# A two-layer gated cross-attention and expert kernel: the maxima are turned ahead of the scores, and routing work changes steps

## The reference

```python
x = x + tanh(g_xattn[0]) * L0_xattn(layernorm(x), ctx, Wq, Wkv, Wo)
x = x + tanh(g_ffn[0])   * L0_ffn(layernorm(x), gate_w, w1, w2)            # top-2 of 8, gelu
x = x + tanh(g_xattn[1]) * L1_xattn(layernorm(x), ctx, ctx, Wq, bq, ...)   # with biases
x = x + tanh(g_ffn[1])   * L1_ffn(layernorm(x), Wr, br, W1, b1, W2, b2)    # top-2 of 8, relu, norm
```

## Time and profile before

| | |
|---|---|
| median of 3 runs | 573.4 us (572.22 to 574.28) |
| the profiled execution's own time | 571.19 us |
| its span, first to last instruction | 569.4 us |
| mean granted TensorE clock | 0.826 of full |
| PE busy | 440.4 us (77%) |
| DVE busy | 336.9 us (59%) |
| ACT busy | 214.2 us (38%) |
| POOL busy | 237.4 us (42%) |
| DMA, mean over the span | 56 GB/s |

### The profile page before, as it was taken

The page is one execution under the profiler, slowest core; times in us unless marked ns, Lnnn a source line. Parts: engine busy times, 40 slices in busy tenths (PEclk is TensorE's granted clock), DMA queues, the critical chain, the costliest instruction groups (busy, mean ns, idle before and its releaser), DMA issues.

```text
span 569.4 us, 16851 instructions
## 1 busy us (share of the span) xinstructions
PE 440.4 (77%) x5346; PEld 334.9 (59%) x5350; DVE 336.9 (59%) x1255; ACT 214.2 (38%) x608; POOL 237.4 (42%) x378
## 2 busy tenths in 40 slices
PE   7788889878576899999478787877865799999300
PEld 4465455545444699998145555544544699999300
DVE  4678556755438656666338855754544756666493
ACT  4434323232232444442044432323221566666221
POOL 7023543453443144445102354435345244554456
PEclk9599785978855999999869968677875999999855
DMA  7791000000000122221200010000010122222241
GB/s 222 213 314 22 21 20 2 22 21 20 20 18 25 47 67 67 70 65 52 74 10 21 20 39 30 4 18 21 20 50 28 42 57 68 63 68 65 70 121 55
DMA packets 38672, 32.06 MB, mean 56 GB/s; under 512 B 6984, under 2 KB 32245, under 8 KB 38613
## 3 DMA queue, kind: packets, MB, share of 16 engines
q1 hardware_dynamic: 34069, 21.86, 14.0%
q0 software_dynamic: 4544, 9.41, 5.1%
HBM read 20.26 MB, written 10.99 MB: 55 GB/s over the span
## 4 chain that ended last, share of the span: by engine, by line
PE 53%; DVE 20%; issue 8%; another core or an unknown queue 8%; ACT 3%; POOL 3%; DMA 2%; DVEq 1%; POOLq 1%; ACTq 0%; SPq 0%
PE bank L671 49%; PE bank L674 4%; DVE room L1288 4%; DVE mx L1265 4%; ACT room L1052 2%; DVE room L1295 1%; DMA o_rows<-room,ids 1%; DVE v_s L1167 1%; POOL wa L648 1%; DVE x L1250 1%; DVE x L1302 1%; DVE wa L1497 1%; DVE fstats L1307 1%; DVE wa L1490 1%
## 5 line engine op out<-in xcount | busy, mean ns | idle before, releaser
L623 POOL DMA_INDIRECT o_rows<-room,ids x78 | 77.7, 996 | 101.0 <-DVE room L1438 37.2
L671 PE MATMUL bank<-room 128*128 128x128 f32 x624 | 83.8, 277 | 2.9 <-issue 2.0
L671 PE MATMUL bank<-wa,room 128*128 x624 | 83.0, 276 | 1.3 <-ACT room L1110 1.1
L671 PEld LDWEIGHTS bank<-room 128*128 128x128 f32 x624 | 75.7, 192 | 6.1 <-ACT room L1115 3.1
L671 PEld LDWEIGHTS bank<-wa,room 128*128 128x128 f32 x624 | 76.1, 192 | 2.0 <-issue 1.9
L576 POOL DMA_INDIRECT xg_rows<-xfa,slots x64 | 63.9, 998 | 32.0 <-issue 19.0
L1265 DVE TENSOR_REDUCE mx<-bank 128x4 f32<-128x324 f32 x128 | 54.4, 487 | 36.2 <-PE bank L671 36.2
L988 ACT ACTIVATE room<-bank 128x128 f32<-128x128 f32 (+1 forms) x110 | 31.2, 284 | 107.2 <-PE bank L674 104.7
L1288 DVE RECIPROCAL room<-bank 128x128 f32<-128x128 f32 x32 | 30.6, 956 | 60.6 <-remote 47.4
L1052 ACT ACTIVATE room<-bank 128x384 f32<-128x384 f32 x128 | 52.4, 495 | 27.0 <-PE bank L671 27.0
L1415 DVE COPY room<-wa 128x512 f32 x78 | 33.3, 427 | 39.2 <-issue 20.3
(11 more groups left out here) (191 smaller groups left out, 733.9 us busy)
## 6 DMA issues: line engine op xcount, KB each, us to landing
room<-xg_rows SPq DMA_DIRECT2D x78, 65.5 KB
wa<-in_L_ffn_w SPq DMA_DIRECT2D x1, 2048.0 KB, 10.1
wb<-in_L_ffn_W SPq DMA_DIRECT2D x1, 2048.0 KB, 17.1
ob<-o_rows SPq DMA_DIRECT2D x32, 64.0 KB, 1.9
wb<-o_rows SPq DMA_DIRECT2D x6, 256.0 KB, 4.5
o_rows<-room,ids POOLq DMA_INDIRECT x78
x<-in_x SPq DMA_DIRECT2D x4, 256.0 KB, 4.4
xg_rows<-xfa,slots POOLq DMA_INDIRECT x64
```

Source lines behind the costliest of these rows:

```text
L623: pool.indirect_dma_start(out=o_dram[l], in_=o_sb[t.slot(UN)][:, :], in_offset=None, out_offset=bass.IndirectOffsetOnAxis(ap=ids[t.slot(UN ...
L671: return pe.matmul(out_, lhsT, rhs, start=start, stop=stop)
```

## The change

On PE: `turn_max` now stands ahead of `scores`, and `less_max` right behind it; the transpose of `xn` stands ahead of `wo`; logits and more_values stand behind `wo`; ranks are made in even steps. On DVE: `ons` directly follows the reciprocal; the ranks and the logits are read out of bank 7 early in the step, and `place` (even steps) and `choose` (odd steps) stand at its end; the later values of a step are kept in the next step; both statistics of a pair are taken together in the even step. On POOL: a pair is scattered at s = b+8 (odd) and no more at b+7 (even); the pair 13 stays at s = 20 and the pair 15 at s = 21, now both through `placed`. The core of the diff:

```diff
+        def due(s, n, last):
+            if s.c == B - 1 + last:
+                return Step(B - 1)
+            return Step(s.c - n) if live_pair(s.back(n)) and s.c - n < B - 1 else None
+        def chosen(s):
+            return due(s, 6, 5)
+        def placed(s):
+            return due(s, 7, 6)
@@ POOL step (in front: xfa of the pair s-4 in odd steps, rstd in even steps)
-                    if live_pair(b6):
+                    if placed(s):
                         ... cum += mb, twice, behind the wait for rk
-                    ready = b6 if b6.c == B - 1 else b7
-                    if live_pair(ready) and (ready.c == B - 1) == (ready is b6):
-                        S["f4"].wait(pool, ready)
...
+                    for b in [b8] * (live_pair(b8) and b8.c < B - 3) + [placed(s)] * (s.c >= B + 4):
+                        S["f4"].wait(pool, b)
+                        S["f2"].wait(pool, b)
+                        scatter(b, 0)
+                        scatter(b, 1)
@@ PE step
-                    if live_pair(b5):
+                    if placed(s):
+                        ranks(placed(s), s)
+                    if live_pair(b5) and b5.c == B - 1:
                         logits(b5)
-                    if live_pair(b6):
-                        S["f3"].wait(pe, b6, 8)
...
-                    if l == 0:
-                        more_values(s)
                     if live(b2):
+                        turn_max(b2)
                         scores(b2)
-                        turn_max(b2)
+                        less_max(b2)
+                    if live(s):
+                        S["xn"].wait(pe, s)
+                        tr(bank[4][:, NC * T:NC * T + P], xn[s.slot(2)][:, :], P).then_inc(S["t1"].sem, 1)
                     if live(b3):
                         ... wo
-                    if live(b2):
-                        less_max(b2)
...
+                    if live_pair(b5) and b5.c < B - 1:
+                        if placed(s):
+                            S["f4"].wait(pe, placed(s), 1)
+                        if l == 0:
+                            pe.wait_ge(v_kept, min(s.c + 1, B))
+                        logits(b5)
+                    if l == 0:
+                        more_values(s)
                     if live_pair(b4):
                         S["f2"].wait(pe, b4)
                         if l == 0:
-                            pe.wait_ge(v_kept, min(s.c + 2, B))
-                        S["f4"].wait(pe, b4.back(2), 1)
+                            pe.wait_ge(v_kept, min(s.c + 1, B))
+                        if chosen(s):
+                            S["f3"].wait(pe, chosen(s), 1)
@@ DVE step
                         dve.reciprocal(...)
-                    if l == 0 and late_batch(s.c) is not None:
-                        ... values_kept(late_batch(s.c))
                         ... ons
+                    if placed(s):
+                        if chosen(s):
+                            S["lg"].wait(dve, chosen(s))
+                        read_ranks(placed(s))
+                    if chosen(s):
+                        read_logits(chosen(s))
+                    if l == 0 and late_batch(s.c - 1) is not None:
+                        ... values_kept(late_batch(s.c - 1))
                     ... norm statistics of s+2, update of x
+                    if live_pair(b3):
+                        ... bn_stats twice, bn_aggr twice
+                    if placed(s):
+                        place(placed(s))
+                    if chosen(s):
+                        choose(chosen(s))
```

More of the change, by code:

```diff
@@ L864, in logits, with ranks @@
                     ins.then_inc(S["lg"].sem, 1)
+                def ranks(b, s):
+                    S["f3"].wait(pe, b, 8)
+                    S["cu"].wait(pe, b.back(2))
+                    if live_pair(s.back(5)):
+                        S["c2"].wait(pe, s.back(5))
+                    if l == 0 and b.c == 1:
+                        hear(pe, "consts")
+                    r0, r1 = bank[7][:, 272:280], bank[7][:, 280:288]
+                    mm(r0, tri[:, :], mb[:, 0, :], True, False)
+                    mm(r0, onesb[:, :], cum[:, :], False, True)
+                    mm(r1, tri[:, :], mb[:, 1, :], True, False)
+                    mm(r1, onesb[:, :], mb[:, 0, :], False, False)
+                    mm(r1, onesb[:, :], cum[:, :], False, True).then_inc(S["rk"].sem, 1)
                 def step(s):
-                    b1, b2, b3, b4, b5, b6 = (s.back(n) for n in (1, 2, 3, 4, 5, 6))
+                    b1, b2, b3, b4, b5 = (s.back(n) for n in (1, 2, 3, 4, 5))
                     if live(b2):
@@ new lines, in choose @@
+                def choose(b):
+                    f3, two = S["f3"], xfa[:, b.c - 1:b.c + 1, D + 1:D + 3]
+                    if l == 0 and b.c == 1:
+                        hear(dve, "consts")
+                    f3.wait(dve, b, 1)
+                    for j in range(2):
+                        dve.max(top[:, j, :], lg[:, j, :]).then_inc(f3.sem, 1)
+                    f3.wait(dve, b, 3)
+                    for j in range(2):
+                        dve.max_index(topi[:, j, :], top[:, j, :], lg[:, j, :]).then_inc(f3.sem, 1)
+                    f3.wait(dve, b, 5)
+                    dve.tensor_copy(two, topi[:, :, 0:2]).then_inc(f3.sem, 1)
+                    f3.wait(dve, b, 6)
+                    S["f4"].wait(dve, b.back(2))
+                    ohv = oh[:, :, :].rearrange("p (j k) e -> p j k e", k=2)
+                    dve.tensor_tensor(ohv, iota8[:, :].unsqueeze(1).unsqueeze(1).to_broadcast([P, 2, 2, E]),
+                                      two.unsqueeze(3).to_broadcast([P, 2, 2, E]), ALU.is_equal).then_inc(f3.sem, 1)
+                    f3.wait(dve, b, 7)
+                    S["cu"].wait(dve, b.back(2))
+                    dve.tensor_tensor(mb[:, :, :], ohv[:, :, 0, :], ohv[:, :, 1, :], ALU.add).then_inc(f3.sem, 1)
+                    dve.tensor_tensor(gap[:, b.c - 1:b.c + 1], top[:, :, 1], top[:, :, 0], ALU.subtract).then_inc(f3.sem, 1)
@@ new lines, in read_ranks, with place @@
+                def read_ranks(b):
+                    S["rk"].wait(dve, b)
+                    dve.tensor_tensor(rk[:, :, :], bank[7][:, 272:288].rearrange("p (j e) -> p j e", j=2),
+                                      bc3(regoff[:, :], 2), ALU.add).then_inc(S["f4"].sem, 1)
+                def place(b):
+                    f4, c = S["f4"], b.c
+                    f4.wait(dve, b, 1)
+                    dve.tensor_tensor(pick[:, :, :].rearrange("p (j k) e -> p k j e", k=2),
+                                      oh[:, :, :].rearrange("p (j k) e -> p k j e", k=2),
+                                      rk[:, :, :].unsqueeze(1).to_broadcast([P, 2, 2, E]), ALU.mult)\
+                        .then_inc(f4.sem, 1)
+                    f4.wait(dve, b, 2)
+                    with nc.allow_low_precision(reason="row numbers, exact in float32 and int32"):
+                        dve.tensor_reduce(slots[:, c - 1:c + 1, :].rearrange("p j k -> p (j k)"), pick[:, :, :],
+                                          AX.X, ALU.add).then_inc(f4.sem, 1)
@@ L1303, in step @@
                                                  ALU.mult, ALU.add).then_inc(S["x2"].sem, 1)
[L1304 removed]
+                    if live_pair(b3):
+                        f1 = S["f1"]
                         S["x2"].wait(dve, b3)
[L1306 to L1311 removed]
```

95 lines of the change are left out of this document (25 added, 70 removed).

## The result

The changed kernel takes **530.46 us** (median of 4 runs, 528.16 to 537.93) where the kernel before takes 573.19 beside it (4 runs, 572.22 to 574.28): ratio **0.924**, 95% interval 0.919 to 0.930. The forecast was 565 (552 to 579); the sign is right, the size is five times too small. The profiled execution is the longest of the four: 537.93, span 535.9, against 571.19 and 569.4. Stretches are read from it. They add up to 7.5 us more than the median tells.

A forecast was written before the change was run, and what follows sets the result against it. Attention was taken as bound by a PE, DVE and ACT chain, its PE part paid at two clocks, with holds at scatters. Layer 0 -5.4 and layer 1 -3.4, together -8.8 from 573.4, gave 565 us, range 552 to 579.

The forecast's parts named there:

- the hold: While POOL issues scatters, PE's results reach other engines late, coming free about 1.0 us behind the last scatter.
- the steps with a scatter: Attention: scatters start about 3.5 us in; only the exponentials wait; next step at 10.4 against 10.77, bounds 8 and 12.
- the exponentials escape: Faster rival, chance 0.13: in scatter steps the exponentials run before the hold; a pair costs 16.5, total 549 us.
- pairs: Two attention steps, one with a scatter: forecast 18.4 us in layer 0 and 18.5 in layer 1.
- s = 17 to `frs` of pair 15: Last scatter step plus clean s = 18: 10.1 and 5.4 us in layer 0, 10.4 and 5.2 in layer 1.
- First steps: Clean steps s = 3 to 7: earlier turn saves 0.7 us each in layer 0, 0.55 in layer 1; -3.5 and -2.7.
- Clean steps between scatters: Attention steps without scatter: early rank reads take 8.5 us to about 8.0 in layer 1, bounds 7.6 and 8.5.
- The tail: After `frs` of pair 15: an extra scatter group costs +3.7 us in layer 0 and +7.5 in layer 1.
- POOL's `rstd` behind four scatters: `rstd` for the next steps queues behind four scatters: costed at nothing, up to 1 us a pair if steps are shorter.
- The slower rival: Chance 0.20: scatter steps beginning at 1.2 GHz let the hold catch the turn; next step at about 11.9, total 580 us.
- does not come from the scatters: Rival, chance 0.07: the hold belongs to PE's own queue at even steps; pairs keep their 10.8 step, about 560 us.

The follow-up runs named there:

- the turn alone: Kernel before with only the maxima turned ahead of the scores and less_max behind them: 556.54 us, ratio 0.970; on another chip 506.43, ratio 0.982.
- the deferred kernel: Changed kernel with all scatters of pairs 1 to 11 held back to step 20: 557.99 us, ratio 0.970; on another chip 550.57, ratio 1.079.

## Why the prediction was wrong

**The step that failed is the place of the hold's beginning, in "the steps with a scatter".** I took it within about 1 us of the first indirect DMA: reciprocal and turn would be out, the exponentials stand behind it, 10.4 for the step. In the traces the lateness grows through the row of four. What PE ends 0.8 behind the first still gets out, 0.6 to 2.0 late; the update of x, whose product ends 1.3 behind, starts 3.5 behind in five of the eight rows of after; most of what PE ends 1.6 or more behind waits for the end of the hold. The odd steps took 7.9 on the mean for 10.4, and this is nearly all of the error in the pairs. The trace of before had both cases, in the step of the earlier trace rows, in rows that I did not weigh (ACT and PE there):

```profile
348.73 1.10 POOL L576 DMA_INDIRECT xg_rows<-xfa,slots  x1 [0.46 <-issue]
349.09 0.49 PE L671 MATMUL bank<-xnT,wq 128*128 128x128 f32 x2
349.50 0.86 PE L671 MATMUL bank<-room,keep 128*32 128x128 f32 x24
...
350.82 0.37 ACT L1064 ACTIVATE room<-bank,bqs 128x128 f32<-128x128 f32 x1 [2.76 <-PE bank L671]
...
351.33 0.63 PE L671 MATMUL bank<-room,kz 32*128 32x128 f32 x9 [0.43 <-issue]
```

The query product ends at 349.58, 0.85 behind the first scatter, and ACT has it at 350.82, in the midst of the row of four and 1.24 late; the weights end at 350.36, 1.63 behind, and are the ones held to 354.62. My own sum put the end of less_max at 0.9 behind the scatter, so by these rows it escapes. That is the rival "the exponentials escape", and its chance of 0.13 should have been the forecast's. On the profiled scale the forecast was 562.4 and 537.7 came (span and 1.8), 24.7 less: pairs -21.1 (58.8 and 67.7 for 73.6 and 74.0), s = 17 to `frs` of pair 15 -4.0 (13.6 and 13.5 for 15.5 and 15.6), first steps -3.1, tails +2.4, small terms about +1. The rival's 16.5 a pair was near in layer 1 (mean 16.9, granted clock 0.81) and too high in layer 0 (14.7, clock 0.88).

**First steps**: right in mechanism, -3.9 and -5.4 for -3.5 and -2.7. 5.48 for 5.7; the bound of 0.85 was passed by a little (0.92), since less_max starts 0.77 behind the scores (41.63, 42.40) and not 0.88. In layer 1 two steps of before that last 8.3 and 7.6 went down to 6.6 and 5.5 as well.

**Clean steps between scatters**: 8.0 was forecast and 7.9 came, by luck, because the hold has moved into these steps. The wait of the earlier trace rows is gone, and the turn alone shows what it would have cost (0.83).

**The tail**: the sum is near, +13.6 for +11.2, the split is wrong. In layer 0 I let PE's keys and values hide the group; they are held themselves, as the products of 0.72 us above are, and end at 159.4: +8.7, above my bound of +5, where the chip without the hold shows +3.5. In layer 1 `cum` of pair 15 comes 13.7 behind its `frs` (forecast 16.1, though the parts listed there add up to 15.6): no hold shows in that tail, and pair 13 is placed at 399.8, while the scatters of pair 11 run.

**POOL's `rstd` behind four scatters**, costed at nothing: on chips without the hold it is what ends the even step (2.46 of wait, some 1.6 a pair). In the profiled run of the changed kernel ACT has no such wait in the steps with the hold.

**The slower rival** did not come, though its condition did. The steps of 328.31 and 362.47 begin at 1.2 GHz (their first product takes 1.46) and last 10.5 and 10.4, not 11.9: the turn gets out, its copy starts 2.1 behind the first scatter, and the exponentials are what is caught. This is my forecast's own picture of a step, and it holds in two of the eight pairs, where PE is late; the other six odd steps last 7.0 on the mean. The clock did not fall at each hold either. Windows of after, the step of 60.97 and the hold behind it (columns as in the earlier trace rows):

```profile
60.97:67.00 6.03, 5.33 (x126) 3.55 (x117) 5.66 (x25) 2.50 (x8) 4.65 (x6) 1.00 0.06 17
67.00:71.00 4.00, 2.80 (x33) 1.30 (x33) 1.03 (x6) 1.18 (x4) 3.20 (x6) 1.00 0.16 51
71.00:75.45 4.45, 4.05 (x93) 3.09 (x92) 4.21 (x14) 2.19 (x7) 0.65 (x4) 1.00 0.00 0
```

1.00 in the step, in the hold and behind it, where the earlier trace rows have 0.50 behind it. This is one pair; layer 1 as a whole gained only 0.02.

**The rival "does not come from the scatters"** is refuted by the deferred kernel: without scatters in the steps there is no hold in them. The rule of the Trainium skill that spoke for it ("Trainium Architecture — The Big Picture", section "What this means for kernel authors": on the engines' side only DVE and GpSimd contend) was answered too quickly in the prediction: the reader that stalls in the earlier trace rows is DVE, one of the two engines that the rule names. What the rule leaves without an explanation is PE, whose 48 products took 10.9 us for 1.01 while POOL issued indirect DMAs. No run shows on which path this happens, so the rule is neither confirmed nor refuted.

## What to carry to other kernels

When a wait ends at a fixed distance behind some transfer, look for its beginning as well: the last thing that the held engine did freely. Where the interval lies in the step is worth more than its length. Before moving a burst to a better place, try to break it up: indirect DMAs one at a time between POOL's other work gave 0.872 where the moved burst gave 0.927. Before a long wait is called a stall, look for the same wait where the stall is absent: one of 22.83 was there without it, and longer. And measure on more than one chip: the gain of this change is 7.3 to 7.6% where the hold shows and 2.6% on one that does not.

## What the runs showed of the hardware

- On the chips where the kernel before takes 573, four indirect DMAs in a row (4.9 us) make PE's work late in the steps. What PE ends 0.8 behind the first is read 0.6 to 2.0 late, and all twelve reciprocals of before start 0.8 to 1.1 behind the last one's end. The first gap of "issue" on PE comes 1.3 behind the first at the earliest, mostly 2 to 4.
- With 28 in a row, 48 products took 10.9 us for 1.01 in layer 0. In the tail of layer 1, 28 and four in a row brought no such wait.
- Two in a row leave waits of 1.4 to 2.4 on the mean. Single ones, most of them 2.0 us or more from start to start, leave none in the steps; a pair in layer 0 takes 12.0 for 11.7.
- The runs on which the kernel before takes 573.2, 573.3 and 573.9 show this, the two chips with 515.4 and 514.9 do not. An indirect DMA takes the same 0.96 us on POOL, with 0.30 between two, on both kinds.
